# A transposed load of x with late centring, and the low parts of projections and numerators exchanged between VectorE and GpSimd, in a two-layer graph attention kernel

## What is computed

```
h = relu(layernorm(x))                             # no affine part
for layer in (0, 1):
    a     = softmax(h @ h.T / sqrt(384))
    delta = a * adj;  attn = delta / (sum(delta) + 1e-10)
    hl, hs, hr = h @ Wl.T + bl, h @ Ws.T + bs, h @ Wr.T + br
    ctx = (attn * upper) @ hl + diag(attn) * hs + (attn * lower) @ hr
    h   = relu(layernorm(ctx) * ln_w + ln_b)
out = x + h
```

## Time and profile before

| | |
|---|---|
| median of 3 runs | 1205.67 us (1205.63 to 1206.1) |
| the profiled execution, its own time | 1205.1 us |
| its span, first to last instruction | 1203.4 us |
| TensorE busy | 1188.6 us, 99% |
| VectorE busy | 917.2 us, 76% |
| ScalarE busy | 528.6 us, 44% |
| GpSimd busy | 560.2 us, 47% |
| mean granted TensorE clock | 0.998 of full speed |

### The profile page before, as it was taken

One profiled execution on the slowest core, in us unless ns is written; L12 is line 12 of the kernel. 1 busy time (PEld: TensorE's weight loads), 2 busy tenths in 40 slices (PEclk: granted clock), 3 DMA queues, 4 the chain that ended last, 5 costly groups with the idle time before them and its releaser, 6 DMA issues.

```text
span 1203.4 us, 18980 instructions
## 1 busy us (share of the span) xinstructions
PE 1188.6 (99%) x7178; PEld 1177.4 (98%) x7178; DVE 917.2 (76%) x2034; ACT 528.6 (44%) x1125; POOL 560.2 (47%) x624
## 2 busy tenths in 40 slices
PE   9999999999999999999999999999999999999997
PEld 7899999999999999999999999999999999999997
DVE  6577995689955899558985599865998659976688
ACT  5346433355333554334544444444344453444532
POOL 4465353454534545335553354442545424554346
PEclk9999999999999999999999999999999999999999
DMA  8001320012200131002310013100231002210000
GB/s 306 21 21 37 109 83 1 1 62 89 79 1 1 62 114 54 1 1 62 114 54 1 1 62 114 53 1 1 69 108 53 1 2 89 87 53 1 1 28 27
DMA packets 37004, 60.87 MB, mean 51 GB/s; under 512 B 2352, under 2 KB 27952, under 8 KB 36912
## 3 DMA queue, kind: packets, MB, share of 16 engines
q1 hardware_dynamic: 36624, 59.26, 15.0%
q10 hardware_dynamic: 288, 0.39, 0.1%
HBM read 47.06 MB, written 12.58 MB: 50 GB/s over the span
## 4 chain that ended last, share of the span: by engine, by line
PE 73%; DVE 10%; ACT 9%; DMA 3%; POOL 2%; issue 2%; DVEq 0%
PE rot_ps L284 13%; PE rot_ps L286 13%; PE rot_ps L285 13%; PE u_ps L284 11%; PE u_ps L286 11%; PE u_ps L285 10%; DMA x_norm<-x_dram 3%; PE rot_ps L348 2%; ACT x_norm L426 2%; ACT e_sb L467 2%; PE u_ps L340 1%; ACT et_hi L481 1%; DVE u_ps L630 1%; ACT hw_hi L477 1%; ACT x_norm L500 1%
## 5 line engine op out<-in xcount | busy, mean ns | idle before, releaser
L881 POOL TENSOR_TENSOR hw_lo<-proj,hw_hi 128x384 fp32r<-128x384 f32 x256 | 280.1, 1111 | 318.8 <-ACT hw_hi L477 318.8
L284 PE MATMUL rot_ps<-w_hi,ht_hi 128*128 128x384 f32 x1152 | 389.7, 338 | 1.3 <-DVE proj L651 1.3
L286 PE MATMUL rot_ps<-w_hi,ht_lo 128*128 128x384 f32 x1152 | 385.6, 335 | 0.0
L285 PE MATMUL rot_ps<-w_lo,ht_hi 128*128 128x384 f32 x1152 | 385.1, 334 | 0.0
L284 PEld LDWEIGHTS rot_ps<-w_hi,ht_hi 128*128 128x128 f32 x1152 | 216.5, 188 | 1.8 <-DVE proj L651 1.6
L452 ACT ACTIVATE u_off<-u_ps 128x128 f32<-128x128 f32 (+1 forms) x128 | 42.5, 332 | 398.8 <-PE u_ps L286 398.6
L285 PEld LDWEIGHTS rot_ps<-w_lo,ht_hi 128*128 128x128 f32 x1152 | 216.6, 188 | 0.0
L286 PEld LDWEIGHTS rot_ps<-w_hi,ht_lo 128*128 128x128 f32 x1152 | 216.2, 188 | 0.0
L651 DVE TENSOR_TENSOR proj<-rot_ps,bias 128x384 f32<-128x384 f32 x256 | 138.2, 549 | 70.7 <-PE rot_ps L286 68.8
L477 ACT ACTIVATE hw_hi<-proj 128x384 fp32r<-128x384 f32 x256 | 126.5, 520 | 77.0 <-DVE proj L651 76.4
L893 POOL TENSOR_TENSOR dg<-et_hi,tri 128x256 fp32r<-128x256 f32 x128 | 103.6, 809 | 121.0 <-PE u_ps L286 121.0
(11 more groups left out here) (89 smaller groups left out, 2055.1 us busy)
## 6 DMA issues: line engine op xcount, KB each, us to landing
out_dram<-z SPq DMA_DIRECT2D x64, 192.0 KB, 1.9
x_norm<-x_dram SPq DMA_DIRECT2D x15, 768.0 KB, 4.4
adj_a<-adj_t_dram SPq DMA_DIRECT2D x8, 1024.0 KB, 5.4
adj_b<-adj_t_dram SPq DMA_DIRECT2D x8, 1024.0 KB, 5.4
x_a<-x_dram SPq DMA_DIRECT2D x8, 768.0 KB, 4.5
x_b<-x_dram SPq DMA_DIRECT2D x8, 768.0 KB, 4.6
w_stage<-w_t_dram SPq DMA_DIRECT2D x4, 576.0 KB, 5.4
e_sb<-w_t_dram SPq DMA_DIRECT2D x1, 576.0 KB, 5.0
```

The costliest lines, as they stand in the source:

```text
L284: pe.matmul(dst, a_hi, b_hi, start=first and m == 0, stop=False)
L285: pe.matmul(dst[:, 0:b_lo.shape[1]], a_hi, b_lo, start=False, stop=False)
L286: done = pe.matmul(dst, a_lo, b_hi, start=False, stop=last and m == n - 1)
L881: pool.tensor_tensor(hw_lo[:, t, n, :], proj[:, t % 2, n, :], hw_hi[:, t, n, 0:dim].bitcast(F32), ALU.subtract).then_inc(hw_lo_done, 1)
```

## The change

**x comes in turned.** A second copy of x, transposed on the host, is an input (`x_t`). For every graph but the first, `load_xt` brings it into a new tile `xt_sb` (384 features as three blocks `db` of 128 partitions, 512 nodes wide). The rows of x are still loaded into `x_norm` (`load_stat_rows`, now four neighbouring rows to a partition), but only for the statistics. The mean and the power of each row lie together in `x_mv`; `store_x_rows` writes them to DRAM, and `spread_x_rows` reads them back to all 128 partitions into the memory of `x_norm`, as `mean_b` and `rstd_b`. GpSimd subtracts the mean (`x_centre`, three of 128x512, behind `rstd_of` in steps 1 and 3), VectorE rectifies and multiplies by the power (`x_scale`, three, at the end of step 0's projections for b and at the start of step 2 for the next a), ScalarE rounds (`round_x`), and VectorE writes the low part (`x_low`, three, among the `finish` of steps 0 and 2).

**Units.** The T units of steps 0 and 3 and `x_normalise` are gone, except for graph 0. Steps 1 and 2 keep theirs. The statistics of both next graphs move to step 1 of VectorE. `ht_f32` now lies in the memory of `proj`, so that `round_h` waits for all eight `hw_lo`.

**The exchange.** `e_low` moves from VectorE to GpSimd, ahead of `triangles(0)`, and `proj_low` from GpSimd to VectorE.

The diff, cut to its core (VectorE, GpSimd, TensorE's units, SyncE):

```diff
-    UNITS_0 = [("P", *p) for p in PROJ + SELF] + TURN
-    UNITS_1 = [("P", *p) for p in PROJ[:4]] + [("M",)] + [("P", *p) for p in PROJ[4:] + SELF] + TURN
-    ORDERS = [UNITS_0, UNITS_0, UNITS_1, UNITS_1]
+    UNITS_0 = [("P", *p) for p in PROJ + SELF]
+    UNITS_1 = [("P", *p) for p in PROJ[:4]] + [("M",)] + [("P", *p) for p in PROJ[4:] + SELF]
+    ORDERS = [UNITS_0, UNITS_0 + TURN, UNITS_1 + TURN, UNITS_1]
...
-        ht_f32 = x_norm[:, :, :].rearrange("p t n -> p (t n)").rearrange("p (k n) -> p k n", n=n_rows)
+        ht_f32 = proj[:, :, :, :].rearrange("p a b d -> p (a b d)").rearrange("p (k n) -> p k n", n=n_rows)
...
             def pair(it, first, last):
+                if not last:
+                    sp.wait_ge(xt_scaled, KB * (next_a - 1))
+                    load_stat_rows(next_a)
+                    sp.wait_ge(ht_lo_done, LEAD_T + at(it, 0, KB, N_H))
+                    load_xt(next_a)
...
+                if not last:
+                    sp.wait_ge(x_stats_done, next_a * XS + TILES)
+                    load_stat_rows(next_b)
+                    store_x_rows(next_a)
+                    store_x_rows(next_b)
+                    spread_x_rows(next_a)
...
+                if not last:
+                    sp.wait_ge(xt_scaled, KB * next_a)
+                    spread_x_rows(next_b)
...
+                def x_scale(graph, db):
+                    dve.wait_ge(xt_centred, KB * (graph - 1) + (db + 1))
+                    dve.scalar_tensor_tensor(out=xt_sb[:, db, :], in0=xt_sb[:, db, :], scalar=0.0, in1=rstd_b,
+                                             op0=ALU.max, op1=ALU.mult).then_inc(xt_scaled, 1)
...
+                def proj_low(t):
+                    for n in range(2):
+                        dve.wait_ge(hw_hi_done, at(it, s, 2 * t + (n + 1), EIGHT))
+                        dve.tensor_tensor(hw_lo[:, t, n, :], proj[:, t % 2, n, :],
+                                          hw_hi[:, t, n, 0:dim].bitcast(F32), ALU.subtract).then_inc(hw_lo_done, 1)
...
+                if s == 1 and not last:
+                    x_stats_of(next_a, range(TILES))
+                    x_variance(next_a)
+                if s == 2 and not last:
+                    for db in range(KB):
+                        x_scale(next_a, db)
                 if layer == 0:
                     evacuate(0, 0)
                     mask(0)
                     evacuate(0, 1)
                     mask(1)
                     mask(2)
                     evacuate(1, 0)
                     mask(3)
-                    e_low(0)
                     evacuate(1, 1)
-                    e_low(1)
-                    e_low(2)
+                    proj_low(0)
                     evacuate(2, 0)
-                    e_low(3)
...
+                    proj_low(1)
+                    evacuate(2, 1)
+                    if s == 1 and not last:
+                        x_stats_of(next_b, range(0, 2))
+                    evacuate(3, 0)
+                    if s == 1 and not last:
+                        x_stats_of(next_b, range(2, TILES))
+                    proj_low(2)
+                    evacuate(3, 1)
+                    if s == 1 and not last:
+                        x_variance(next_b)
                     diagonal(0)
                     diagonal(1)
+                    evacuate(0, 2)
+                    proj_low(3)
+                    for t in range(1, TILES):
+                        evacuate(t, 2)
+                    for t in range(2, TILES):
+                        diagonal(t)
                 else:
...
                     shift_scores(0)
+                    proj_low(0)
                     shift_scores(1)
                     evacuate(2, 0)
                     shift_scores(2)
                     shift_scores(3)
+                    proj_low(1)
                     mask(0)
                     evacuate(2, 1)
                     mask(1)
                     mask(2)
+                    evacuate(3, 0)
                     mask(3)
+                    evacuate(3, 1)
+                    proj_low(2)
                     evacuate(0, 2)
+                    proj_low(3)
+                    for t in range(1, TILES):
+                        evacuate(t, 2)
                     for t in range(TILES):
                         diagonal(t)
...
+            def x_centre(graph):
+                pool.wait_ge(xt_loaded, 16 * graph)
+                pool.wait_ge(x_rows_spread, 16 * graph)
+                for db in range(KB):
+                    pool.tensor_tensor(xt_sb[:, db, :], xt_sb[:, db, :], mean_b, ALU.subtract).then_inc(xt_centred, 1)
...
-                proj_low(0)
+                if s == 1 and not last:
+                    x_rstd_of(it * 2 + 2)
                 set_ones()
-                proj_low(1)
...
+                for t in range(TILES):
+                    e_low(t)
+                triangles(0)
+                if s == 1 and not last:
+                    x_rstd_of(it * 2 + 3)
+                triangles(1)
...
                 rstd_of(slice(0, TILES), 1)
-                if s >= 2 and not last:
-                    x_rstd_of(it * 2 + (s + 1))
+                if s in (1, 3) and not last:
+                    x_centre(it * 2 + (2 if s == 1 else 3))
```

More of the change, by code:

```diff
@@ L11, with build_digcn @@
 P = 128
[L14 removed]
+def build_digcn(nc, x, x_t, adj_t, w_t, bl, bs, br, ln_w, ln_b, ln_w0_t, ln_b0_t, out):
     n_graphs, n_rows, dim = x.shape
@@ L172, in build_digcn @@
         x_norm_loaded = sem("x_norm_loaded")
+        x_rows_stored = [sem(f"x_rows_stored_{g}") for g in "ab"]
+        x_rows_spread = sem("x_rows_spread")
+        xt_loaded = sem("xt_loaded")
+        xt_centred = sem("xt_centred")
+        xt_scaled = sem("xt_scaled")
         x_loaded = [sem(f"x_loaded_{g}") for g in "ab"]
@@ L247, in _ @@
             sp.dma_start(beta[:, :], ln_b[1:2, :].to_broadcast([P, dim])).then_inc(vec_loaded, 16)
-            for g in range(2):
-                sp.dma_start(x_sb[g][:, :, :], rows(x, g)).then_inc(x_loaded[g], 16)
+            sp.dma_start(x_sb[0][:, :, :], rows(x, 0)).then_inc(x_loaded[0], 16)
             sp.wait_ge(w_lo0_done, KB)
@@ L541, in step @@
                     round_e(3)
[L542 to L545, removed]
                 round_proj(3)
-                if first and s == 0:
-                    x_normalise(2, range(TILES))
-                if not final:
+                if s in (1, 2):
                     for db in range(KB):
                         round_h(db)
+                if s == 0 or (s == 2 and not last):
+                    for db in range(KB):
+                        round_x(db)
                 if first and s == 0:
@@ L605, in step, with x_stats_of @@
                 g, layer = s % 2, s // 2
-                early = first and s == 0
-                ahead = None if last else {2: it * 2 + 3, 3: it * 2 + 4}.get(s)
+                next_a, next_b = it * 2 + 2, it * 2 + 3
+                def x_stats_of(graph, tiles):
+                    if tiles[0] == 0:
+                        dve.wait_ge(x_norm_loaded, 16 * graph)
+                    for t in tiles:
+                        x_statistics(t)
+                def x_scale(graph, db):
+                    dve.wait_ge(xt_centred, KB * (graph - 1) + (db + 1))
+                    dve.scalar_tensor_tensor(out=xt_sb[:, db, :], in0=xt_sb[:, db, :], scalar=0.0, in1=rstd_b,
+                                             op0=ALU.max, op1=ALU.mult).then_inc(xt_scaled, 1)
                 def row_max(t):
@@ L716, in aggregate @@
                     dve.bn_aggr(mv[:, i, :], stats[:, i, :]).then_inc(aggr_done, 1)
+                if first and s == 0:
+                    x_stats_of(1, range(TILES))
+                    x_variance(1)
+                if s == 1 and not last:
[4 more added lines that the diff above has]
+                        x_scale(next_a, db)
                 if layer == 0:
@@ L807, in step @@
                         centre(i - 1)
-                    if ahead is not None and i in (1, 2):
-                        if i == 1:
-                            dve.wait_ge(x_norm_loaded, (ahead - 1) * 16)
-                        x_statistics(2 * i - 2)
-                        x_statistics(2 * i - 1)
+                    if s == 0 and i < 2:
+                        for db in ((0,), (1, 2))[i]:
+                            x_low(next_a - 1, db)
+                    if s == 2 and not last and i in (1, 2):
+                        for db in ((0, 1), (2,))[i - 1]:
+                            x_low(next_a, db)
                 dve.wait_ge(stats_done, at(it, s, TILES, FOUR))
@@ L876, in set_ones, with e_low @@
                     pool.memset(hs[:, :, dim:EXT], 1.0).then_inc(ones_done, 1)
-                def proj_low(t):
-                    for n in range(2):
-                        pool.wait_ge(hw_hi_done, at(it, s, 2 * t + (n + 1), EIGHT))
-                        pool.tensor_tensor(hw_lo[:, t, n, :], proj[:, t % 2, n, :],
```

(5 more changed lines are left out.)

208 lines of the change are left out of this document (92 added, 116 removed).

## The result

The change makes the kernel slower: 1229.56 us (median of 4 runs, 1228.62 to 1232.76) against 1205.65 us, a ratio of 1.0202 (95%: 1.0183 to 1.0222). The forecast was 1240 in a range of 1196 to 1258. The side is right, and the loss of 23.9 us is seven tenths of the 34.4 that I had forecast. The profiled execution of the changed kernel took 1232.76 us, the longest of the four.

A forecast was written before the change was run, and what follows sets the result against it. TensorE, busy 99% of the span, was taken to bound the kernel. Seven steady pairs at +5.0 us, with the first and last pair's corrections, made +35.0 on 1205.1: 1240 us, range 1196 to 1258.

The forecast's parts named there:

- The limit of the gain: T units removed from TensorE plus the wait in step 3: at most about 23 us gained, so 1182 us.
- The port as the hidden price: VectorE instructions with two SBUF inputs and GpSimd's take turns; `e_low` takes 0.68 us alone, 1.28 beside `proj_low`.
- step 0: `x_centre` takes turns with `affine` and `add_x`, making evacuations late; less the T units removed: +1.0 us.
- step 1: `proj_low` takes turns with `e_low`; `evacuate(1, 2)` ends at 26.9 and delays T units and `attend(0)`: +2.0 us.
- step 2: `x_scale` alternates with `x_centre`, then `proj_low` takes turns; T unit 1 waits for its bank: +2.7 us.
- step 3: T units and an old wait go, but `attend(0)` is late for the last `hw_lo`: -0.7 us.
- the pair: Sum of the four steps of a steady pair: +5.0 us, seven times 35.0.
- the length of the turns: VectorE's waits for GpSimd: 4.2 us in step 1, 2.7 in step 2, 3.5 in step 0.
- Rival 1: Turns fall apart, so VectorE reaches `evacuate(1, 2)` in time: 1182 to 1203 us; chance 0.2.
- Rival 2: Centring by `x_centre` and `x_scale` comes late; two us beyond six of delay would give 1254 us; chance 0.06.
- Rival 3: TensorE's clock falls from 2.4 to 1.2 GHz after one gap in each pair: 32 us, so 1272; chance 0.04.
- theory A: The forecast's view: turns since the exchange delay TensorE through `evacuate(1, 2)`; for the exchange alone, 1222 to 1230 us.

The follow-up runs named there:

- experiment 3: Changed kernel with each `proj_low` on VectorE replaced by an equally wide instruction with one SBUF input, leaving `hw_lo` zero: 1178.39 us.
- experiment 5: Changed kernel without the exchange (transposed x only), with `x_centre` of graph b moved from the end of step 3 to step 0: 1180.41 us.
- Experiment 2: Kernel before with the exchange alone, including the changed kernel's order on VectorE and GpSimd: 1242.27 us.
- experiment 6: Changed kernel with only `x_centre` of graph b moved from the end of step 3 to step 0, behind `triangles(1)`: 1224.51 us.
- experiment 4: Changed kernel with `evacuate(1, 2)` and `evacuate(2, 2)` put ahead of `proj_low(3)` in layer 0 and step 2: 1209.82 us.

## Why the prediction was right, and where its size was off

**The limit of the gain: right.** I put the change without turns at 1182 us. Experiments 3 and 5, in which in two different ways no turn reaches TensorE any more, gave 1178.4 and 1180.4. That is 2 to 4 us less than the limit, since TensorE's waits in the first step go as well, which the limit left out.

**The port as the hidden price: right, and shown.** I read it from one pair of instructions in the earlier trace rows. It holds over 256: experiment 3 replaces `proj_low` alone, by an instruction without the second input, and the times of both become constant and the loss a gain. The Trainium skill (SBUF — State Buffer, section on the two separate sides) has the lock against VectorE instructions with two SBUF inputs or in a two-port mode, and against no others; the 530 to 553 ns of the form with one input, beside 534 to 1652 with two, agree.

**The steps: right in place and sign.** Forecast against measured, from the change's windows and those of the earlier trace rows: step 0 +1.0 and +0.5 to 0.6; step 1 +2.0 and +1.3; step 2 +2.7 and +2.2; step 3 -0.7 and -1.2 (-1.0 by the first score products); the pair +5.0 and +2.9. The waits are where the forecast had them, at `hs` in steps 1 and 2 and at `proj` in step 0. Seven pairs make 20.5 of the span's 27.6 us; the clock (below) makes 4.6, and the first step, the last pair and the tail the rest: step 2 of the last pair costs 1.75 as forecast (1.8), the first step 0 gains only 1.5 where I had 2.3.

**What was off: the length of the turns.** The forecast priced `e_low` at 1.25 us and every turn at its whole length, 4.2 us of waits in step 1, 2.7 in step 2 and 3.5 in step 0. Measured, they are (2.25 + 2.67 + 1.47) - 6 x 0.47 = 3.6 in step 1 (the rows above, less 0.07 of overlap each), 2.3 in step 2 and 3.0 in step 0. `e_low` by itself was priced right (1.29). But from its start to the next one's, with a `proj_low` between, 1.57 us pass (518.99 to 522.13 holds two), not 1.25 + 0.47 = 1.72: a turn of VectorE's costs GpSimd 0.3 us and not its full 0.47. The earlier trace rows held a sign of it: there 0.60 us of VectorE's made GpSimd's next longer by 0.45. So GpSimd's four are through earlier, and the last `proj_low` pairs meet it for less. `evacuate(1, 2)` ends at 26.2 in step 1 (forecast 26.9) and at 27.6 in step 2 (28.4; there the first `shift_scores` was also 0.4 earlier than I had it, 13.9). In the steps' lengths that is 0.4 to 0.7 us less in each of the four, together the difference between 5.0 and 2.9 a pair. (Two of the forecast's losses also don't follow to the tenth from its own times: 26.9 - 25.1 is 1.8 and not 2.0, 28.4 - 25.6 is 2.8 and not 2.7.) My median for `hw_lo` (near 1 us) was high for the same reason and one more: in layer 1 four of its eight come while GpSimd is idle.

**Rival 1, the turns fall apart: no.** In step 1 its point of decision was 2.4 us of turns; 3.6 were there. **Rival 2, late centring: no.** TensorE never waits for it (only in the first pair, once, 0.5 us for an `x_low`), and the transfers land well inside the 9.4 us assumed:

```profile
xt_sb<-x_t_dram SPq DMA_DIRECT2D x15, 768.0 KB, 4.6
x_norm<-rows_dram SPq DMA_DIRECT2D x15, 512.0 KB, 3.7
rows_dram<-x_mv SPq DMA_DIRECT2D x15, 4.0 KB, 2.7
```

**Rival 3, the clock: it came, but small.** I had given it 0.04 and said that nothing showed it. In the profiled execution it happened three times. TensorE's time line around the first, and two windows there:

```profile
418.69 1.12 PE L400 MATMUL rot_ps<-ident,z 128*128 128x128 f32 x8 [1.84 <-DVE hs L711]
...
420.26 0.53 PE L337 MATMUL u_ps<-hw_hi,et_hi 128*128 128x386 f32 x1
...
423.84 0.34 PE L337 MATMUL u_ps<-hw_hi,et_hi 128*128 128x386 f32 x1
```

```profile
420.00:424.00 4.00, 4.00 (x15) 4.00 (x15) 2.82 (x11) 3.88 (x7) 0.13 (x1) 0.57 0.01 4
424.00:428.00 4.00, 4.00 (x24) 4.00 (x24) 2.42 (x6) 0.00 (x0) 2.70 (x4) 1.00 0.00 0
```

After a gap of 1.84 us in step 2 the granted clock is 0.57 for the 4 us from 420, products take 0.53 us instead of 0.34, and 15 are done where 24 fit. Where products take the longer time the clock is at its lower level, 1.2 GHz, and else at 2.4 GHz. It costs 1.5 us each time (a step 2 of 40.8 instead of 39.25), 4.6 in all, and hides a part of my overestimate: without it the profiled execution's loss would be 23 us. The other three executions, with mean granted clocks of 0.995, 0.996 and 0.996 against its 0.994, took 1230.26, 1228.62 and 1228.86 us. Experiment 2, whose gaps in step 3 are 2.0 to 2.1 us, has three falls. But the next pair has the same gap at the same place (until 570.96, 1.83 us), and there the clock stays:

```profile
571.00:575.00 4.00, 4.00 (x26) 3.95 (x27) 3.73 (x13) 3.90 (x7) 1.62 (x4) 1.00 0.01 4
```

All falls within the work come behind gaps of 1.8 to 2.0 us, but most such gaps have none: only three of seven have one here and one of seven in experiment 6. Behind the gaps of 2.1 and 2.2 us in experiment 2 and of 2.2 us in experiment 4 the clock stayed. What decides is open; no experiment was made on it. The profiled execution of experiment 2, which theory A had put lower, is 35.7 us longer than before. Steps 2 and 3 of seven pairs make 7 x (1.8 + 1.6) = 24 of them, the three falls and the one step of 40.88 us 4 x 1.6 = 6, and most of the rest is what theory A had left out: 1.9 in step 1 of the first pair, 1.8 and 0.8 in steps 2 and 3 of the last, and 1.0 behind TensorE's last product.

## What to carry to other kernels

Before work is moved between VectorE and GpSimd, list which of VectorE's instructions read two operands from SBUF, and lay both engines' time lines over each other: beside GpSimd's they add up for the most part instead of running side by side, even where each engine alone has spare time. Then look whose wait ends last, and put what TensorE wants (here two evacuations of 0.47 us) ahead of what takes turns; that order alone was worth 20 us. And test the parts of a compound change by themselves: one of these two gained 25 us once its centring was placed where VectorE has time to wait for it, the other alone cost 37.

## What the runs showed of the hardware beyond what was expected

A turn is not paid in full by both sides: `e_low` on GpSimd takes 1.29 us alone and 1.60 with a 0.47 us instruction of VectorE in between, while VectorE waits out the whole of GpSimd's (two `proj_low` of 1.01 us take up to 2.74). A narrow instruction of VectorE's waits as long as a wide one: `shift`, on 128 x 4, takes 1244 to 1250 ns in the seven steps 2 where it meets `x_centre`, and else 161 to 164:

```profile
L885 DVE SCALAR_TENSOR_TENSOR shift<-mv,rstd x16: 161/164/1250, 54.2 to 1149.8; 128x4 f32<-128x4 f32 x16
```

And the granted clock of TensorE fell to its lower level behind three of the seven gaps of 1.84 us, at 1.5 us lost each time, and behind none of the longer ones, of 2.1 to 2.2 us, in experiments 2 and 4.
